# Counting the first pair of node tiles inside the preparation block of a graph network kernel

## The chip, the cores and the metric

The kernel runs on one NeuronCore of a Trainium2 chip. The time is device microseconds (us) of one launch, as the median of several runs. The five engines have their own instruction queues, each strictly in order: TensorE (PE in the profile; its weight loads are PEld), VectorE (DVE), ScalarE (ACT), GpSimd (POOL) and SyncE (SP, which here only starts DMAs). They meet at semaphores alone.

## The reference

6250 nodes with 256 features, 200000 edges sorted by destination, two graph-convolution layers and then a mixture of six experts (top 2). Cut to what the change touches:

```python
x = x + _L0_gnn_ref(_layernorm(x, axis=-1), edge_index, W, b, resW, resb)
...
deg = segment_sum(ones, dst); dis = rsqrt(deg); norm = dis[src] * dis[dst]   # self loops included
for l in range(2):
    h = x @ W[l]
    agg = segment_sum(norm[:, None] * h[src], dst) + b[l]
    x = relu(agg + x @ resW + resb)
```

## The kernel before, in words

The nodes are 49 tiles of 128 (`tiles`, padded to 50), taken two at a time as 25 `pairs`. The gather and the segment sum are done as a product of dense matrices: for each pair the kernel builds a matrix of edge counts (source node by destination node) and multiplies it with all messages, which stay in SBUF as two 16-bit parts (`parts`, a high part and the rest).

**The preparation block** (lines 755 to 1214, one `nc.Block`) does, for every tile `t` in two loops of 49, the work before the first layer's sums.

- The residual loop. VectorE gets the row statistics of a group of tiles (`stats`), ScalarE subtracts the mean in place (`centre`, L852), TensorE turns the tile (`turn`, L934), ScalarE copies it back (`turned_copy`, L862), TensorE multiplies with the residual weight (`residual`, L942) into one of four PSUM banks, and VectorE scales and stores it (`residual`, L1038). TensorE's tile `t` waits for VectorE's tile `t - 4`.
- The message loop. TensorE multiplies the turned tile with the layer's weight (`message`, L953, four PSUM banks), ScalarE writes the high part (`high`, L879), VectorE the rest (`rest_of`, L1045), ScalarE that rest as the second part (`middle`, L883). TensorE's message `t` waits for VectorE's `rest_of(t - 4)`.
- The keys. GpSimd fetches each tile's edge list by 49 indirect DMAs (L835). VectorE makes float keys in five batches of ten tiles, each in six steps (`key_step(n, step)`, L1058 to L1073; step 2 lets TensorE turn them, step 5 gives the node degrees). TensorE turns them pair by pair (`turn_keys`, L963), ScalarE copies them out as `keys_t` (`keys_copy`, L866) and takes the roots of the degrees (`roots`, L870, the first one in ScalarE's iteration 36).

All of this stands in a hand-written order: lists such as `STATS_AFTER`, `KEYS_AFTER_RES` (key batches 0 and 1 turned after residuals 34 to 38 and 44 to 48), `KEYS_AFTER_H` (batches 2 to 4 after messages 9, 17 and 27 on), `NORMS_BEFORE`, `FLAG_AFTER_H` say behind which tile a step is queued. `flag_and_bounds` is a chain of some 18 tiny VectorE instructions after `rest_of(37)`.

**The counting block** (`count_and_sum`, L1476 on) follows after a block boundary at which all engines meet. For each pair VectorE makes one-hot rows in 8 steps of 16 nodes (`rows_of_step`: a `rows_lo` and a `rows_hi` comparison, both at L623), TensorE counts them in 32 `quads` of four 128x98 matmuls (`build`, L1479), ScalarE copies each quad to `counts` (L1559). From the second pair on this runs beside the sums of the pair before (`sum_units`, L1404: 100 matmuls of 128x512 a pair). The first pair has nothing to run beside: its 32 quads stand ahead of the first sum.

The tile `counts` has two halves. In the preparation block the same memory holds the centred and turned features `feat`, so its first half comes free when message 24 is done.

Of the kernel before, what the change touches and what calls it, by code (L numbers as in the profile page):

```python
# [18 lines left out]
P = 128  # L19
# [460 lines left out]
def gnn_moe_kernel(nc, x, src, dst, gnn_w, gnn_b, res_w, res_b, router_w1, router_b1, router_w2, router_b2,  # L480
# [35 lines left out]
    with ctx:  # L516
# [92 lines left out]

        open_scope()  # L610
# [53 lines left out]
        assert 2 * pairs % BATCH == 0 and BATCH % 2 == 0  # L664

# [61 lines left out]
        middle_ready = sem("middle_ready")  # L727

# [4 lines left out]
        NORMS_BEFORE = 24  # L733
        STATS_AFTER = (16, 20, 26, 32)

        KEYS_AFTER_RES = (34, 44)
# [15 lines left out]
        def h_bank(t):  # L752
            return bank[(2, 3, 0, 1)[t % 4]]

# [3 lines left out]
        with nc.Block() as block:  # L758
# [39 lines left out]
            def _(pool):  # L798
# [14 lines left out]
                nc.gpsimd.iota(iota_hi[:, :, :], [[1, width], [0, 2]], 0, 0, allow_small_or_imprecise_dtypes=True)  # L813
# [35 lines left out]
            def _(act):  # L849
# [35 lines left out]

                act.wait_ge(cleared, 4)
# [4 lines left out]
                for t in range(tiles):  # L891
                    if t + 2 < tiles:
                        centre(t + 2)
                        if group_of(t + 2) != group_of(t + 1):
                            deviations(group_of(t + 2))
# [5 lines left out]
                    if t >= 4 and keys_after_res(t - 4) is not None:  # L901
                        keys_copy(keys_after_res(t - 4))
# [4 lines left out]
                for t in range(tiles - 4, tiles):  # L907
# [13 lines left out]
            def _(pe):  # L921
# [43 lines left out]

                count_heads(0)
# [23 lines left out]
                for t in range(tiles):  # L990
# [3 lines left out]
                    if t == FLAG_AFTER_H:  # L994
                        pe.wait_ge(disorder_ready, 1)
                        nc.tensor.matmul(bank[6][:, 0:3], ones[:, :], disorder[:, :], start=True, stop=True).then_inc(ones_summed, 1)

            @block.vector
            def _(dve):
# [135 lines left out]
                def flag_and_bounds():  # L1135
                    dve.wait_ge(ones_summed, 5)
                    link(nc.vector.tensor_reduce(over[:, 0:1], bank[6][:, 0:3], AX, ALU.add))
# [9 lines left out]
                    for l in range(layers):  # L1147
                        link(nc.vector.tensor_scalar(dis_back[:, l, :], dis[:, :], power[:, 1, l:l + 1].bitcast(F32), None, ALU.mult))

# [35 lines left out]
                for t in range(16, tiles):  # L1185
# [14 lines left out]
                for t in range(tiles):  # L1200
# [11 lines left out]
                    if t == 37:  # L1212
# [173 lines left out]
        QUAD = 4  # L1386
        quads = P // QUAD
        UNITS = 2 * (tiles + 1)
        LAST_UNITS = tiles + 1
        half_bank = 2  # L1390
# [1296 lines left out]
```

## Time and profile before

| | us |
|---|---|
| median of 3 runs (1899.73 to 1903.38) | 1903.04 |
| profiled execution | 1904.81 |
| its span in the trace | 1902.7 |
| residual loop starts, on TensorE | 18.79 |
| message loop starts, on TensorE | 120.49 |
| first counts matmul (pair 0) | 177.13 |
| first sum matmul of the first layer | 193.88 |

TensorE is busy for 1820.8 us, 96% of the span, VectorE for 1124.2 us, ScalarE for 853.7 us, GpSimd for 340.8 us. TensorE's granted clock, in tenths, over 40 slices of 47.6 us is 9988 and then 9 in all of the rest. A row of the view by stretch gives the busy time of each engine between two times, with the number of instructions in brackets, then the granted clock (1.00 is 2.4 GHz, 0.50 is 1.2 GHz), the busy share of the DMA engines and their GB/s. A row of the view in order of time gives start, length, engine, line, operation, tiles and shapes, how many instructions are merged in it, and in square brackets how long the engine sat idle before and what released it. A row of the groups by line gives the count, the busy time and the mean of one in ns.

### The profile page before, as it was taken

The numbers are of one execution on the slowest core, as the hardware profiler recorded it, in microseconds if no ns is written. First come the engines' busy times: TensorE is split into PE (matmuls) and PEld (weight loads), VectorE is DVE, ScalarE is ACT, GpSimd is POOL, SyncE is SP. The second block draws the span as 40 slices with busy tenths as digits, with TensorE's granted clock in tenths as the row PEclk, the third lists the DMA queues.
The fourth block names the chain that finished last, engine by engine and source line by source line (L and its number), as shares of the span: only waits on it lengthen the run. The fifth ranks groups of instructions, "written<-read, shape, count | busy, mean of one in ns | idle before, by whom it ended". The sixth has DMA issues, their size and how long they took to land. (4 is left out here: it accounts for less than half of the span.)

```text
span 1902.7 us, 35412 instructions
## 1 busy us (share of the span) xinstructions
PE 1820.8 (96%) x11170; PEld 1120.5 (59%) x11170; DVE 1124.2 (59%) x2789; ACT 853.7 (45%) x1822; POOL 340.8 (18%) x347
## 2 busy tenths in 40 slices
PE   4887999999999999999999999999999999999996
PEld 3666555555555555555544444444444478888885
DVE  7867666676666666766514444444444568555553
ACT  2567555555555555656512222222222232556562
POOL 1780000000000000000001111111111124333332
PEclk9988999999999999999999999999999999999998
DMA  7377999889999989898284555444445479324441
GB/s 216 99 129 133 327 300 318 288 289 284 292 286 288 257 305 347 328 323 306 104 338 179 190 179 188 179 179 179 179 179 182 180 232 335 111 77 122 141 135 55
DMA packets 135978, 416.70 MB, mean 219 GB/s; under 512 B 13685, under 2 KB 81611, under 8 KB 129640
## 3 DMA queue, kind: packets, MB, share of 16 engines
q1 hardware_dynamic: 90376, 255.13, 38.8%
q0 software_dynamic: 45392, 160.65, 28.8%
q8 instruction: 31, 0.51, 0.1%
q14 instruction: 35, 0.29, 0.1%
q10 hardware_dynamic: 144, 0.13, 0.0%
HBM read 162.27 MB, written 262.07 MB: 223 GB/s over the span
## 5 line engine op out<-in xcount | busy, mean ns | idle before, releaser
L1404 PE MATMUL bank<-parts,counts 128*128 128x512 f16 x4704 | 1158.4, 379 | 0.9 <-DVE sums L1425 0.9
L1404 PEld LDWEIGHTS bank<-parts,counts 128*128 128x128 f16 x4704 | 416.1, 97 | 358.0 <-issue 2.8
L1559 ACT ACTIVATE counts<-bank 128x392 f16<-128x392 f32 x800 | 394.7, 497 | 313.3 <-PE bank L1479 306.5
L623 DVE TENSOR_TENSOR rows<-rows,iota_lo 128x2048 bf16<-128x2048 bf16 x200 | 244.9, 1224 | 237.5 <-PE bank L1479 237.1
L1479 PEld LDWEIGHTS bank<-rows 128*128 128x128 bf16 x3200 | 229.7, 99 | 202.8 <-issue 27.6
L1479 PE MATMUL bank<-rows 128*128 128x98 bf16 x3200 | 280.5, 211 | 9.5 <-DVE rows L623 8.6
L623 DVE TENSOR_TENSOR rows<-rows,iota_hi 128x1568 bf16<-128x1568 bf16 x200 | 193.5, 968 | 0.0
L467 POOL DMA_INDIRECT first_rows<-route_rows,route_spot_i x49 | 47.8, 976 | 580.6 <-DVE tokens L458 405.0
L1419 ACT ACTIVATE middle<-bank 128x256 f32<-128x256 f32 x98 | 37.1, 380 | 187.0 <-PE bank L1404 172.2
L2187 PE MATMUL bank<-y_t,counts 128*128 128x256 f32 x480 | 114.4, 382 | 3.0 <-ACT y_t L2259 3.0
L2187 PE MATMUL bank<-h_t,counts 128*128 128x256 f32 x480 | 114.2, 381 | 0.0
L2216 PE MATMUL bank<-counts,h_t 128*128 128x256 f32 x480 | 113.5, 380 | 0.0
L2401 DVE TENSOR_SCALAR h_t<-bank,counts 128x256 f32<-128x256 f32 x120 | 57.8, 481 | 87.6 <-PE bank L2187 87.6
L2187 PEld LDWEIGHTS bank<-y_t,counts 128*128 128x128 f32 x480 | 91.3, 191 | 16.2 <-issue 3.7
L2263 ACT ACTIVATE h_t<-bank,counts 128x256 f32<-128x256 f32 x120 | 56.0, 467 | 98.5 <-PE bank L2187 89.0
L388 DVE TENSOR_TENSOR route_prob<-bank,router_b_sb 128x12 f32<-128x12 f32 (+1 forms) x25 | 4.2, 170 | 161.9 <-PE bank L378 161.9
L2216 PEld LDWEIGHTS bank<-counts,h_t 128*128 128x128 f32 x480 | 90.8, 190 | 12.2
L2288 ACT ACTIVATE counts<-parts 128x514 f32 x135 | 92.4, 700 | 9.0 <-issue 2.5
L2187 PEld LDWEIGHTS bank<-h_t,counts 128*128 128x128 f32 x480 | 87.2, 191 | 9.6
L183 PE MATMUL bank<-both_w,rows 128*128 128x512 f32 x196 | 92.2, 593 | 0.0
L2492 POOL DMA_INDIRECT first_out<-both_w,to_row x60 | 60.5, 1009 | 128.4 <-DVE both_w L2414 116.9
L2492 POOL DMA_INDIRECT out_dram<-both_w,to_row x60 | 58.3, 971 | 104.9 <-DVE both_w L2414 94.8
(268 smaller groups left out, 1761.1 us busy)
## 6 DMA issues: line engine op xcount, KB each, us to landing
counts_table<-counts SPq DMA_DIRECT2D x25, 3136.0 KB, 15.0
counts<-counts_table SPq DMA_DIRECT2D x24, 3136.0 KB, 11.7
first_rows<-zero_rows POOLq DMA_DIRECT2D x3, 10530.0 KB, 59.4
second_rows<-zero_rows POOLq DMA_DIRECT2D x3, 10449.0 KB, 69.6
first_out<-zero_rows POOLq DMA_DIRECT2D x3, 10368.0 KB, 50.5
res_tile<-res_table SPq DMA_DIRECT2D x98, 128.0 KB, 7.4
first_rows<-zero_rows POOLq DMA_DIRECT2D x1, 10270.0 KB, 60.4
second_rows<-zero_rows POOLq DMA_DIRECT2D x1, 10191.0 KB, 68.1
```

The costliest lines, as they stand in the source:

```text
L183: mm = nc.tensor.matmul(self.product_bank[:, :], self.x1_t[:, o, k * P:(k + 1) * P], self.both_w[:, self.l + 1, k, :], start=k == 0, stop= ...
L467: pool.indirect_dma_start(table, bass.IndirectOffsetOnAxis(ap=self.spot_i[:, b, c, o:o + 1], axis=0), rows[:, b, o, lo:hi], None, bounds_c ...
L623: return nc.vector.tensor_tensor(rows, k, v, ALU.is_equal)
L1404: mm = nc.tensor.matmul(acc[:, 0:2 * dim], lhs, rhs, start=s == 0, stop=s == tiles)
L1479: mm = nc.tensor.matmul(bank[4 + q % 4][:, u * width:(u + 1) * width], rows_lo[:, r % 2, at, :, u % 2], rows_hi[:, r % 2, at, :, u % 2], s ...
L1559: nc.scalar.activation(counts[:, b, :, :].rearrange("p s (o n) -> p o s n", o=2)[:, :, :, q * QUAD:(q + 1) * QUAD], bank[4 + q % 4][:, 0:Q ...
L2187: mm = nc.tensor.matmul(to[m][:, 0:ROWS], weights_of(k, n)[:, kf, m * P:(m + 1) * P], source[:, k % 2, kf, :], start=kf == 0, stop=kf == K ...
L2216: mm = nc.tensor.matmul(outs_bank[k % 2][:, cols_of], h2_t[:, k % 2, kf, h * P:(h + 1) * P], weights_of(k, 2)[:, kf, :], start=kf == 0, st ...
L2263: nc.scalar.activation(to[:, k % 2, 0, :], frm[0][:, 0:ROWS], ACT.Relu, bias=bias_of(k, n, 0)).then_inc(low_out, 1)
L2288: nc.scalar.activation(w[:, k % WB, part], held[:, bass.ds(e, 1), part].rearrange("p a n -> p (a n)"), ACT.Copy).then_inc(w_loaded[n][k % ...
L2401: nc.vector.tensor_scalar(to[:, k % 2, 1, :], frm[1][:, 0:ROWS], bias_of(k, n, 1), 0.0, ALU.add, ALU.max).then_inc(high_out, 1)
L2492: pool.indirect_dma_start(table, bass.IndirectOffsetOnAxis(ap=to_row[:, k % SB, h:h + 1], axis=0), result[:, k % 2, cols_of], None, bounds ...
```

## The change

The 32 quads of pair 0 move out of the counting block into the message loop of the preparation block: TensorE counts one or two of them behind each of the messages 25 to 45 into banks 6 and 7, ScalarE copies them between `high(t)` and `middle(t - 1)`, two messages later in TensorE's order than its own, and VectorE makes the eight one-hot steps behind `rest_of` of tiles 6, 14, 16, 24, 27, 30, 33, 36 (first comparison) and one tile later (second), in four buffers, two of them in the memory of edge lists that are no longer needed. In the counting block the copy loops begin with pair 1, and TensorE does 12 sum matmuls before the first quad of pair 1 (`SUMS_AHEAD`).

In the residual loop the key steps, the disorder check and the norms come three or four tiles earlier on VectorE, the turning of key batches 0 and 1 five tiles earlier on TensorE, and ScalarE's copy of turned keys, which stood behind `turned_copy(t)` four tiles later, stands two tiles later in front of `centre(t + 2)`. The flag's matmul goes to another bank and waits for the key copies; the flag's VectorE chain moves from behind tile 37 to behind tile 40. The amount of arithmetic is the same.

```diff
-        NORMS_BEFORE = 24
-        STATS_AFTER = (16, 20, 26, 32)
+        NORMS_BEFORE = 20
+        STATS_AFTER = (16, 20, 25, 31)
-        KEYS_AFTER_RES = (34, 44)
+        KEYS_AFTER_RES = (29, 39)
+        FREE_AFTER = -(-tiles // 2)
+        COUNT_FOR = tiles - FREE_AFTER - 3
+        AHEAD = 2
+        ROW_BUFS = 4
+        def quads_after(t):
+            return range(*(min(max(n, 0), COUNT_FOR) * quads // COUNT_FOR for n in (t - FREE_AFTER, t + 1 - FREE_AFTER)))
+        def quad_bank(q):
+            return bank[6 + q % 2]
+        ONEHOTS_AFTER_H = (6, 14, 16, 24, 27, 30, 33, 36)
...
# ScalarE
                 for t in range(tiles):
+                    if t >= 2 and keys_after_res(t - 2) is not None:
+                        keys_copy(keys_after_res(t - 2))
                     if t + 2 < tiles:
                         centre(t + 2)
...
-                    if t >= 4 and keys_after_res(t - 4) is not None:
-                        keys_copy(keys_after_res(t - 4))
...
                     high(t)
+                    if keys_after_h(t) is not None:
+                        keys_copy(keys_after_h(t))
+                    for q in quads_after(t + AHEAD):
+                        quad_copy(q)
                     if t >= 1:
                         middle(t - 1)
-                    if t >= 1 and keys_after_h(t - 1) is not None:
-                        keys_copy(keys_after_h(t - 1))
...
# TensorE
+                def count_quad(q):
+                    r, u0 = divmod(q * QUAD, STEP)
+                    if u0 == 0:
+                        pe.wait_ge(onehots_made, r + 1)
+                    if q >= 2:
+                        pe.wait_ge(quad_out, q - 1)
...
                     if t == FLAG_AFTER_H:
                         pe.wait_ge(disorder_ready, 1)
-                        nc.tensor.matmul(bank[6][:, 0:3], ones[:, :], disorder[:, :], start=True, stop=True).then_inc(ones_summed, 1)
+                        pe.wait_ge(keys_out, pairs - 1)
+                        nc.tensor.matmul(bank[5][:, 2 * P:2 * P + 3], ones[:, :], disorder[:, :], start=True, stop=True).then_inc(ones_summed, 1)
+                    for q in quads_after(t):
+                        count_quad(q)
...
# VectorE
+                def pair_heads(r):
...
+                    if r >= ROW_BUFS:
+                        dve.wait_ge(quad_ready, (r - ROW_BUFS + 1) * per_step)
+                    onehot_rows(lo_rows[r % ROW_BUFS], keys_t[:, 0, 1, r * STEP:(r + 1) * STEP], iota_lo, STEP, P)
+                def pair_tiles(r):
+                    onehot_rows(hi_rows[r % ROW_BUFS], keys_t[:, 0, 0, r * STEP:(r + 1) * STEP], iota_hi, STEP, width).then_inc(onehots_made, 1)
...
-                    if t == 22:
+                    if t == 18:
                         disorders()
-                    if t == 25:
+                    if t == 21:
                         norms()
-                    if 27 <= t < 33:
-                        key_step(0, t - 27)
-                    if 37 <= t < 43:
-                        key_step(1, t - 37)
+                    if 24 <= t < 30:
+                        key_step(0, t - 24)
+                    if 34 <= t < 40:
+                        key_step(1, t - 34)
...
+                    if t in ONEHOTS_AFTER_H:
+                        pair_heads(ONEHOTS_AFTER_H.index(t))
+                    if t - 1 in ONEHOTS_AFTER_H:
+                        pair_tiles(ONEHOTS_AFTER_H.index(t - 1))
-                    if t == 37:
+                    if t == 40:
                         flag_and_bounds()
...
# the counting block
+        SUMS_AHEAD = 12
...
                 def sum_pair(i, b, first, last=False):
                     pe.wait_ge(quad_out, i * quads + quads)
                     units = LAST_UNITS if last else UNITS
+                    ahead = SUMS_AHEAD if first else 0
+                    if first:
+                        sum_units(pe, b, i, i, 0, ahead, update.sums_out, update.sums_ready, first)
...
-                for q in range(quads):
-                    build(q, 0, True)
                 sum_pair(0, 0, True)
...
-                for i in range(4):
+                for i in range(1, 4):
                     pair(i, i % 2)
```

## Rows read from the trace of the kernel before

**Rows 1.** Busy time of each engine by stretch (us from the span's start)

```profile
64.60:97.00 32.40, 26.81 (x134) 20.76 (x132) 30.27 (x94) 16.50 (x44) 25.36 (x24) 1.00 0.36 104
92.00:120.50 28.50, 21.81 (x104) 17.43 (x102) 16.56 (x45) 11.90 (x35) 23.01 (x26) 0.82 0.35 96
121.00:150.00 29.00, 27.13 (x132) 22.01 (x131) 25.60 (x57) 22.61 (x65) 21.86 (x33) 1.00 1.06 140
177.00:193.50 16.50, 11.89 (x128) 10.20 (x128) 16.47 (x19) 13.33 (x32) 1.56 (x1) 0.50 0.90 253
193.50:198.00 4.50, 4.41 (x21) 2.20 (x22) 2.01 (x2) 1.49 (x3) 0.00 (x0) 0.50 1.01 259
193.00:1160.00 967.00, 964.02 (x6756) 523.42 (x6757) 587.08 (x1015) 489.87 (x1082) 65.17 (x39) 1.00 0.83 274
```

**Rows 2.** Order of time on PE: end of the residual loop, first messages

```profile
98.99 0.41 PE L963 MATMUL bank<-ident,node_keys 128*128 128x128 f32 x2 [4.17 <-ACT keys_t L866]
...
111.22 1.03 PE L942 MATMUL bank<-both_w,counts 128*128 128x256 f32 x4
112.08 0.38 PE L934 MATMUL bank<-ident,counts 128*128 128x128 f32 x2
112.30 1.03 PE L942 MATMUL bank<-both_w,counts 128*128 128x256 f32 x4
...
120.49 8.94 PE L953 MATMUL bank<-both_w,counts 128*128 128x256 f32 x40
```

**Rows 3.** Order of time on ACT: what it waits for at tile 36

```profile
97.03 0.21 ACT L870 ACTIVATE dis<-deg 128x10 f32<-128x10 f32 x1 [4.39 <-DVE deg L1073]
```

**Rows 4.** Order of time on DVE: rest of tile 24, the flag's chain

```profile
149.10 0.48 DVE L1045 SCALAR_TENSOR_TENSOR rest<-bank,message_scale,parts 128x256 f32<-128x256 f32 x1
...
161.83 0.15 DVE L1137 TENSOR_REDUCE over<-bank 128x1 f32<-128x3 f32 x1
...
165.39 0.88 DVE L1045 SCALAR_TENSOR_TENSOR rest<-bank,message_scale,parts 128x256 f32<-128x256 f32 x2
```

**Rows 5.** Order of time on ACT: one message, the last one, first quads

```profile
167.56 0.47 ACT L879 ACTIVATE parts<-bank,message_scale 128x256 f16<-128x256 f32 x1
167.91 0.41 ACT L883 ACTIVATE parts<-rest 128x256 f16<-128x256 f32 x1
168.23 0.46 ACT L879 ACTIVATE parts<-bank,message_scale 128x256 f16<-128x256 f32 x1
...
173.30 0.42 ACT L883 ACTIVATE parts<-rest 128x256 f16<-128x256 f32 x1 [0.25 <-DVE rest L1045]
177.67 1.67 ACT L1559 ACTIVATE counts<-bank 128x392 f16<-128x392 f32 x4 [3.95 <-PE bank L1479]
```

**Rows 6.** Groups by line, 0 to 320 us: copies of turned keys

```profile
L866 ACT ACTIVATE keys_t<-bank 128x256 bf16<-128x256 f32 x25 | 9.3, 376 | 1.7 <-PE bank L963 1.7
```

**Rows 7.** Order of time on DVE: start of the counting block

```profile
174.70 0.23 DVE L1523 COPY rows<-keys_t 128x256 bf16<-128x256 bf16 x1 [1.43 <-PEq L758]
174.96 1.23 DVE L623 TENSOR_TENSOR rows<-rows,iota_lo 128x2048 bf16<-128x2048 bf16 x1
...
176.99 1.22 DVE L623 TENSOR_TENSOR rows<-rows,iota_lo 128x2048 bf16<-128x2048 bf16 x1
```

**Rows 8.** Order of time on PE: last messages, first sums, a later quad

```profile
165.93 6.31 PE L953 MATMUL bank<-both_w,counts 128*128 128x256 f32 x28 [1.59 <-DVE rest L1045]
...
193.88 1.48 PE L1404 MATMUL bank<-parts,counts 128*128 128x512 f16 x3
...
210.54 0.35 PE L1479 MATMUL bank<-rows 128*128 128x98 bf16 x4
210.72 0.81 PE L1404 MATMUL bank<-parts,counts 128*128 128x512 f16 x3
```

**Rows 9.** One line's durations on DVE (min/median/max ns): two key steps

```profile
L1063 DVE TENSOR_TENSOR node_keys<-edge_hi,node_base x5: 815/815/817, 88.4 to 143.2; 128x640 f32<-128x640 int32 x5
L1058 DVE TENSOR_SCALAR key_i<-onehot_lo x5: 480/482/609, 87.1 to 141.7; 128x640 int32<-128x640 int32 x5
```

More of the change, by code:

```diff
@@ L608, in rows_of @@
             return table.rearrange("(t p) d -> p t d", p=P)
+        QUAD = 4
+        quads = P // QUAD
+        STEP = 16
+        steps = P // STEP
+        per_step = STEP // QUAD
         open_scope()
@@ L883, in middle, with quad_copy @@
                     nc.scalar.activation(parts[:, t, dim:2 * dim], rest[:, t % 2, :], ACT.Copy, scale=LOW).then_inc(middle_ready, 1)
+                def quad_copy(q):
+                    act.wait_ge(quad_ready, q + 1)
+                    nc.scalar.activation(
+                        counts[:, 0, :, :].rearrange("p s (o n) -> p o s n", o=2)[:, :, :, q * QUAD:(q + 1) * QUAD],
+                        quad_bank(q)[:, 0:QUAD * width].rearrange("p (n o s) -> p o s n", o=2, s=tiles), ACT.Copy).then_inc(quad_out, 1)
                 act.wait_ge(cleared, 4)
@@ L906, in _ @@
                         roots(1)
-                for t in range(tiles - 4, tiles):
+                for t in range(tiles - 2, tiles):
                     if keys_after_res(t) is not None:
@@ L964, in turn_keys @@
                     tr.then_inc(keys_turned, 1)
+                def count_quad(q):
[4 more added lines that the diff above has]
+                        pe.wait_ge(quad_out, q - 1)
+                    for u in range(QUAD):
+                        at = (u0 + u) // 2
+                        mm = nc.tensor.matmul(quad_bank(q)[:, u * width:(u + 1) * width], lo_rows[r % ROW_BUFS][:, at, :, u % 2],
+                                              hi_rows[r % ROW_BUFS][:, at, :, u % 2], start=True, stop=True)
+                    mm.then_inc(quad_ready, 1)
                 count_heads(0)
@@ L1136, in flag_and_bounds @@
                     dve.wait_ge(ones_summed, 5)
-                    link(nc.vector.tensor_reduce(over[:, 0:1], bank[6][:, 0:3], AX, ALU.add))
+                    link(nc.vector.tensor_reduce(over[:, 0:1], bank[5][:, 2 * P:2 * P + 3], AX, ALU.add))
                     link(nc.vector.tensor_scalar(over[:, 0:1], over[:, 0:1], 1.0, None, ALU.min))
@@ L1469, in tensor, with build @@
             def tensor(pe):
-                def build(q, i, first):
+                def build(q, i):
                     r, u0 = divmod(q * QUAD, STEP)
@@ L1474, in build @@
                         pe.wait_ge(onehots_made, i * steps + (r + 1))
-                    if not (first and q < 4):
-                        pe.wait_ge(quad_out, i * quads + (q - 3))
+                    pe.wait_ge(quad_out, i * quads + (q - 3))
                     for u in range(QUAD):
@@ L1509, in vector, with rows_of_step @@
             def vector(dve):
-                def rows_of_step(r, i, b, first):
-                    if not (first and r < 2):
-                        dve.wait_ge(quad_ready, i * quads + (r - 1) * per_step)
+                def rows_of_step(r, i, b):
+                    dve.wait_ge(quad_ready, i * quads + (r - 1) * per_step)
                     nodes_of = slice(r * STEP, (r + 1) * STEP)
@@ L1524, in pair @@
                                           keys_t[:, bass.ds(i, 1), :, :].rearrange("p a k n -> p (a k n)")).then_inc(keys_copied, 1)
-                    dve.wait_ge(keys_copied, i + 1)
+                    dve.wait_ge(keys_copied, i)
                     for r in range(steps):
-                        rows_of_step(r, i, b, isinstance(i, int) and i == 0)
+                        rows_of_step(r, i, b)
                         if there(i * 2 - 4):
@@ L1595, in pair @@
                                 update.high_part(act, i * 2 - 2, 0, i - 1)
-                for i in range(4):
+                for i in range(1, 4):
                     pair(i, i // 2, i % 2)
```

30 lines of the change are left out of this document (19 added, 11 removed).

## The prediction

> **What bounds the kernel now.** I read the stretches first [rows 1]. From 193 to 1160 us TensorE is busy for 964 of 967 us. Nothing in the change touches what stands there, so whatever the change gains or loses ahead of the first sum, which starts at 193.88 [rows 8], should appear unchanged at the end. The question is therefore only when the first sum can start. Ahead of it are three pieces with different limits.
>
> The residual loop ends at 120.49, where the first message starts [rows 2]. From 64.60 to 97.00 VectorE is busy for 30.27 of 32.40 us: it is the bound there, TensorE with 26.81 is not [rows 1]. Then comes a hold that belongs to nobody's work: TensorE sits idle 4.17 us for a copy of turned keys by ScalarE [rows 2], and ScalarE itself sat 4.39 us for the degrees of key batch 0, which VectorE makes behind tile 32 [rows 3]. After that hold the granted clock is low; over 92.0 to 120.5 it is 0.82 on average and TensorE is busy for only 21.81 of 28.50 us [rows 1].
>
> The message loop takes from 120.49 to 173.72, the end of ScalarE's last part (173.30 plus 0.42 [rows 5]). In its first half TensorE (27.13 of 29.0) and VectorE (25.60) are both nearly full [rows 1].
>
> The third piece is pair 0's counts. The counting block starts for VectorE at 174.70 [rows 7], 0.98 after ScalarE's end, and the first sum comes at 193.88. In it VectorE is busy for 16.47 of 16.50 us and TensorE runs at clock 0.50 [rows 1]. That is the piece that the change takes apart.
>
> **Residual loop: earlier by 8.1 us.** The same VectorE instructions stand ahead of tile 32 in both orders, so the full stretch of 30.27 us cannot shrink by more than its 2.1 us of idle time; I let VectorE finish tile 32 at 96 instead of 97. TensorE, which may lead by four tiles, is then at tile 36. The degrees of batch 0 are now made behind tile 29, seven tiles ahead of ScalarE's root at 36 and further back than TensorE's lead, so the 4.39 us hold goes; what is late next is VectorE, until 96. The key copy now stands two iterations behind its turning, ahead of `turned_copy`, so TensorE's next turning of keys no longer waits for a copy that itself waits for TensorE. Queued behind the copy on ScalarE are `centre` and `turned_copy`; their tiles are two ahead of the residual that wants them. From tile 36 on TensorE has 13 residuals with their turning, 1.08 us each (111.22 to 112.30 [rows 2]), 14.0 us, and five key turnings at 0.22 us (a turning, 112.08 to 112.30 [rows 2]), 1.1 us: 111.1 us. I add 1.3 us, because TensorE waits for batch 0's keys once behind tile 29 (an estimate of 2 to 3 us, since VectorE has disorders, norms and two groups of statistics close together there), and such a wait may lower its clock for a while. Messages start at 112.4 instead of 120.49: 8.1 us. Bounds: 10, if the clock never falls; 3, if the clock falls as it did behind the 4.17 us hold and all ten key tiles run slowly.
>
> **Message loop, first half: later by 4.4 us.** Until `rest_of(24)` three one-hot steps are added, 2.03 us each (174.96 to 176.99 [rows 7]), 6.1 us, on an engine that had 3.4 us idle in 29 [rows 1]. Half of that idle time I let them fill: 6.1 less 1.7 is 4.4. So `rest_of(24)`, which started 28.6 us behind the first message (149.10 [rows 4]), starts 33.0 us behind it. Bounds 2.7 (all idle time filled) and 6.1 (none). The fourth step's first half, 1.23 us, already lies beside the next piece.
>
> Here a rule speaks against the change. The rows: GpSimd issues DMAs for 21.86 us of 121 to 150 [rows 1], and the VectorE comparison with two SBUF inputs that is in the trace there, L1063, takes 815 to 817 ns in all five places, while the one-input L1058 goes from 480 to 609 [rows 9]. The Trainium skill ("SBUF — State Buffer", Who interferes with whom and SBUF: two separate sides) says that VectorE and GpSimd share a port pair that is locked for a whole instruction, and that a VectorE instruction with two SBUF inputs is blocked by a GpSimd one that reads SBUF. If each of the six one-hot instructions waited for one GpSimd instruction (21.86 / 33, 0.66 us), this half would be 4 us longer; by L1063 it is nothing, and I take nothing.
>
> **Message loop, second half: later by 7.9 us.** Here ScalarE becomes the bound. One message costs it 0.67 us (167.56 to 168.23 [rows 5]): 24 messages, 16.1 us. The 32 quad copies cost 1.67 / 4 = 0.42 us each [rows 5], 13.4 us. Five key copies of 0.376 us [rows 6] that overlap by a tenth make 1.4 us. The flag's chain holds VectorE for 3.56 us (161.83 to 165.39 [rows 4]) behind tile 40; ScalarE has two messages with three or four quads queued that do not need it, so I count 1.6 us of it. Sum 32.5 us from `rest_of(24)` to the last part, against 173.72 less 149.10, 24.6 us: 7.9 more. TensorE needs 0.89 us a message (8.94 us for ten [rows 2]) and about 1.5 quads of 0.18 us (210.54 to 210.72 [rows 8]), 1.17 us against ScalarE's 1.31, and it runs two messages ahead. VectorE needs 0.4 us plus a one-hot step every third tile, about 1.1 us. So both are cover, not bound; each quad waits for the copy two before it, which ScalarE made one message earlier. The steps for buffers 4 to 7 wait for quads counted at least one message before. Bounds: 5 (VectorE's flag hidden, TensorE's lead intact) and 12, below.
>
> **The block boundary and the first sum: earlier by 19.2 us.** ScalarE ends at 173.7 - 8.1 + 4.4 + 7.9 = 177.9; 0.98 us later, at 178.9, the counting block starts. TensorE now has 12 sums in front, which need no one-hot rows: at 1.48 / 3 or 0.81 / 3 us each [rows 8] 5.9 or 3.2 us, longer than the 0.26 + 2.03 = 2.3 us until pair 1's first rows [rows 7]. So the first sum starts at 178.9 instead of 193.88, and everything behind it is the same work. Its first 4.5 us ran at clock 0.50 [rows 1]; after an idle boundary of two to three us I expect the same again, worth at most 2.2 us if not.
>
> **The sum.** -8.1 + 4.4 + 7.9 - 19.2 = -15.0 us. The profiled execution took 1904.81 us, 1.77 above the median; 1904.8 - 15.0 = 1889.8, and against the median 1903.04 - 15.0 = 1888.0 us. I predict 1888.
>
> **Rivals.** (a) *The hold only moves.* The residual loop stays bound by waits on keys, gaining 3 of 8 us, or the one-hot steps fill no idle time and cost 6.1. For it: 30.27 of 32.40 us on VectorE [rows 1] leave little room. Time 1890 to 1896, about 1893.
> (b) *Quads and copies take turns.* If TensorE cannot get ahead of ScalarE, each quad and its copy stand in series: 32 x (0.18 + 0.50) + 21 x 0.89 = 40.5 us for messages 25 to 45 where the forecast has about 29; 11.5 more, 1899.5, no measurable change. Against it: two banks, and copies placed two messages behind.
> (c) *TensorE's clock stays low in the message loop* (slower than before). Behind the hold of 4.17 us [rows 2] the clock was low for so long that 92.0 to 120.5 averages 0.82 [rows 1], and messages with quads also leave it a little idle. At 1.2 GHz a message takes about 1.75 us and a quad 0.37 (11.89 / 32 [rows 1]); messages 25 to 48 take 24 x 1.75 + 32 x 0.37 = 54 us instead of 32.5, and 1888 + 21 = 1909. It decides from 15 such messages on: each costs 1.75 + 0.56 - 1.31 = 1.0 us, and 15 us is the gain. Against it: at 26.81 busy of 32.40 us the clock was still 1.00 [rows 1], and a slow TensorE would run without gaps.
> (d) *More than forecast:* all idle time filled, no low clock, the flag hidden: 1880 to 1884.
> (e) That the change doesn't do what it says, pair 0's quads still being counted behind the boundary, is excluded by the diff: the loop over them is gone.
>
> **Chances.** Forecast (1884 to 1892) 0.50; (a) 0.19; (d) 0.13; (b) 0.08, split between no change and its neighbours; (c) 0.10. A measurement can tell about 0.2%, 3.8 us. Faster 0.82, same 0.08, slower 0.10. Range: the forecast with (a) and (d) and the bounds above, 1880 to 1897, leaves (b), (c) and little else out.
>
> **What would show it.** In the profile after: no wait of TensorE on `keys_t` above 1 us and the first message at 110 to 115; ScalarE without idle time from message 25 on, with the quad copies between its two parts; the first sum at 176 to 183, at most 1.5 us behind VectorE's key copy; and from there to the end the same length as before, 1708.8 us. Wrong would be: TensorE waiting in every quad for a copy (b), a granted clock under 0.9 over the message loop (c), or a first sum that comes early while the sums of pair 0 wait for one-hot rows.

## The result and the profile after

The changed kernel takes 1891.09 us (median of 4 runs, 1889.59 to 1892.94), beside 1902.87 us for the kernel before on the same chip: a ratio of 0.9941, 95% interval 0.993 to 0.9953. It is 11.8 us faster, 3 us less than the 15 us of the sum. The time alone does not choose between the forecast (1884 to 1892) and rival (a) (1890 to 1896), since it lies in both; the marks below do. The profiled execution took 1892.94 us with a span of 1890.8 us, against 1904.81 and 1902.7 before.

The first reading is a list of marks on TensorE, in us from the start of each span. "First half" runs from the first message to VectorE's `rest_of(24)`, "second half" from there to the end of ScalarE's last part; the last column is the end of the last sum of both layers.

| | first message | first half | second half | first sum | last sum | span |
|---|---|---|---|---|---|---|
| before | 120.49 | 28.61 | 24.62 | 193.88 | 1539.94 | 1902.7 |
| forecast | 112.4 | 33.0 | 32.5 | 178.9 | | |
| after | 114.47 | 32.52 | 36.18 | 184.24 | 1528.32 | 1890.8 |

So the first sum comes 9.6 us earlier, and the sums themselves take 1344.1 us instead of 1346.1: 9.6 + 2.0 = 11.6 us at the last sum. The remaining 0.3 us lie behind it.

Busy time of each engine by stretch of after (columns: span of the stretch; busy us and instructions of PE, PEld, DVE, ACT, POOL; granted clock; DMA share; GB/s). The stretches are the residual loop up to tile 36, its end, the two halves of the message loop, and the boundary with the first sums; they answer to [rows 1].

```profile
64.98:98.90 33.92, 28.24 (x134) 21.71 (x132) 30.50 (x95) 18.29 (x52) 26.17 (x26) 0.95 0.34 102
99.00:114.50 15.50, 15.33 (x85) 13.09 (x86) 11.80 (x27) 9.62 (x28) 11.77 (x13) 1.00 0.47 145
114.50:147.00 32.50, 30.44 (x144) 22.40 (x143) 31.09 (x62) 22.68 (x63) 27.77 (x41) 1.00 0.96 151
147.00:183.20 36.20, 29.30 (x215) 23.45 (x213) 24.86 (x55) 30.51 (x86) 0.00 (x0) 0.95 0.33 50
183.20:188.70 5.50, 4.46 (x31) 2.34 (x32) 4.36 (x5) 1.02 (x3) 3.44 (x1) 1.00 0.70 293
```

Line 2 is the part that went best: TensorE busy for 15.33 of 15.50 us at full clock, where before the 28.5 us ahead of the first message had a clock of 0.82. In line 3 both TensorE and VectorE (31.09 of 32.50) are full. Line 4 is the surprise: no engine is full. ScalarE, which the sum took for the bound, is busy for 30.51 of 36.20 us.

TensorE in order of time, after (start, length, line, tiles; in brackets the idle time before and its releaser):

```profile
66.28 2.07 PE L983 MATMUL bank<-both_w,counts 128*128 128x256 f32 x4 [1.12 <-ACT counts L895]
...
83.91 1.10 PE L983 MATMUL bank<-both_w,counts 128*128 128x256 f32 x4 [2.50 <-DVE parts L1094]
...
90.50 0.44 PE L1004 MATMUL bank<-ident,node_keys 128*128 128x128 f32 x2 [2.02 <-DVE node_keys L1121]
...
99.12 1.10 PE L983 MATMUL bank<-both_w,counts 128*128 128x256 f32 x4 [0.26 <-DVE parts L1094]
...
114.47 9.04 PE L994 MATMUL bank<-both_w,counts 128*128 128x256 f32 x40
...
151.21 0.41 PE L1004 MATMUL bank<-ident,node_keys 128*128 128x128 f32 x2 [0.90 <-ACT keys_t L899]
...
153.52 0.41 PE L1004 MATMUL bank<-ident,node_keys 128*128 128x128 f32 x2 [0.79 <-ACT keys_t L899]
...
156.12 0.41 PE L1004 MATMUL bank<-ident,node_keys 128*128 128x128 f32 x2 [0.89 <-ACT keys_t L899]
...
175.53 2.08 PE L994 MATMUL bank<-both_w,counts 128*128 128x256 f32 x4 [2.25 <-DVE rest L1101]
...
184.24 2.76 PE L1475 MATMUL bank<-parts,counts 128*128 128x512 f16 x12 [2.93 <-PEq L791]
```

The 4.17 us hold on `keys_t` of [rows 2] is gone from the residual loop. A shorter wait on `keys_t` has appeared three times in the message loop. Message 45 waits 2.25 us for VectorE and then runs four matmuls in 2.08 us, twice the 1.09 that its neighbours take: half clock.

ScalarE in order of time, after, at the same places:

```profile
151.84 0.50 ACT L921 ACTIVATE counts<-bank 128x392 f16<-128x392 f32 x1 [0.77 <-PE bank L1015]
...
154.15 0.89 ACT L921 ACTIVATE counts<-bank 128x392 f16<-128x392 f32 x2 [0.77 <-PE bank L1015]
...
156.75 0.50 ACT L921 ACTIVATE counts<-bank 128x392 f16<-128x392 f32 x1 [0.77 <-PE bank L1015]
...
175.50 0.42 ACT L916 ACTIVATE parts<-rest 128x256 f16<-128x256 f32 x1 [1.24 <-DVE rest L1101]
...
177.97 0.89 ACT L921 ACTIVATE counts<-bank 128x392 f16<-128x392 f32 x2 [1.68 <-PE bank L1015]
...
182.75 0.42 ACT L916 ACTIVATE parts<-rest 128x256 f16<-128x256 f32 x1 [0.24 <-DVE rest L1101]
```

And VectorE, after: a one-hot step beside GpSimd's DMA issues, `rest_of(24)`, the flag's chain from its first instruction to the next rest, and the key copy that opens the counting block:

```profile
123.71 1.21 DVE L629 TENSOR_TENSOR pair_lo<-keys_t,iota_lo 128x2048 bf16<-128x2048 bf16 x1
...
146.99 0.48 DVE L1101 SCALAR_TENSOR_TENSOR rest<-bank,message_scale,parts 128x256 f32<-128x256 f32 x1
...
171.42 0.15 DVE L1193 TENSOR_REDUCE over<-bank 128x1 f32<-128x3 f32 x1
...
174.99 0.88 DVE L1101 SCALAR_TENSOR_TENSOR rest<-bank,message_scale,parts 128x256 f32<-128x256 f32 x2
...
184.14 0.23 DVE L1587 COPY rows<-keys_t 128x256 bf16<-128x256 bf16 x1 [1.43 <-PEq L791]
```

### The profile page after: what moved, and what is told of

Same layout as the page of the kernel before. It is cut to its first block and busy times, and to the rows that moved or that the text cites. A ratio compares the mean times of both kernels' runs of the same rounds, so it can differ in the third digit from the quotient of the medians.

```text
span 1890.8 us, 35393 instructions
## 1 busy us (share of the span) xinstructions
PE 1817.2 (96%) x11170; PEld 1115.8 (59%) x11170; DVE 1124.5 (59%) x2788; ACT 852.4 (45%) x1822; POOL 340.2 (18%) x347
## 5 line engine op out<-in xcount | busy, mean ns | idle before, releaser
L1623 ACT ACTIVATE counts<-bank 128x392 f16<-128x392 f32 x768 | 381.7, 497 | 305.4 <-PE bank L1543 298.0
L629 DVE TENSOR_TENSOR rows<-rows,iota_lo 128x2048 bf16<-128x2048 bf16 x192 | 235.3, 1225 | 232.1 <-PE bank L1543 231.6
L1543 PEld LDWEIGHTS bank<-rows 128*128 128x128 bf16 x3072 | 219.0, 98 | 190.7 <-issue 26.8
L1543 PE MATMUL bank<-rows 128*128 128x98 bf16 x3072 | 267.9, 208 | 0.1
L629 DVE TENSOR_TENSOR rows<-rows,iota_hi 128x1568 bf16<-128x1568 bf16 x192 | 186.0, 969 | 0.0
L2478 DVE SCALAR_TENSOR_TENSOR both_w<-bank,rows,both_w 128x256 f32<-128x256 f32 x120 | 52.5, 479 | 43.5 <-PE bank L2280 40.9
```

What stands on the lines that cost most here:

```text
L629: return nc.vector.tensor_tensor(rows, k, v, ALU.is_equal)
L1543: mm = nc.tensor.matmul(bank[4 + q % 4][:, u * width:(u + 1) * width], rows_lo[:, r % 2, at, :, u % 2], rows_hi[:, r % 2, at, :, u % 2], s ...
L1623: nc.scalar.activation(counts[:, b, :, :].rearrange("p s (o n) -> p o s n", o=2)[:, :, :, q * QUAD:(q + 1) * QUAD], bank[4 + q % 4][:, 0:Q ...
L2478: ins = nc.vector.scalar_tensor_tensor(result[:, k % 2, cols_of], outs_bank[k % 2][:, cols_of], rows[:, k % SB, h, gate_at[c]:gate_at[c] + ...
```

## What was still open

Three questions followed from these rows. First, what each half of the change earns alone. Second, why the second half took 36.18 us where 32.5 were forecast. My theory was two separate loops. One is a **key loop**: TensorE turns the keys behind message t + 2 only when the copy of the turning two messages back is out, that copy stands in ScalarE's iteration t, and behind it ScalarE waits for quads that TensorE counts behind that same turning. The other is the **flag's chain**: VectorE's 3.57 us from 171.42 to 174.99 is not covered, as ScalarE's 1.24 and 1.68 us of idle time show. The rival was one common cause, TensorE too slow or its lead too short for all quads (rival (b) of the prediction). Third, why the residual loop gained 6.0 us and not 8.1.

## Experiments on the two halves of the change

**Residual loop alone.** The kernel before, with only the new places of the residual loop: the lists, the key steps, the disorder check and the norms, and the key copy:

```diff
-        NORMS_BEFORE = 24
-        STATS_AFTER = (16, 20, 26, 32)
-        KEYS_AFTER_RES = (34, 44)
+        NORMS_BEFORE = 20
+        STATS_AFTER = (16, 20, 25, 31)
+        KEYS_AFTER_RES = (29, 39)
...
+                    if t >= 2 and keys_after_res(t - 2) is not None:
+                        keys_copy(keys_after_res(t - 2))
...
-                    if t >= 4 and keys_after_res(t - 4) is not None:
-                        keys_copy(keys_after_res(t - 4))
...
-                    if 27 <= t < 33:
-                        key_step(0, t - 27)
+                    if 24 <= t < 30:
+                        key_step(0, t - 24)
...
```

> The kernel before with only the new order of the residual loop (keys, norms, disorder check, key copies); pair 0 is still counted behind the block boundary. Theory: the parts add up; in the profile of the changed kernel the first message starts at 114.47 us instead of 120.49, so this kernel should start its messages at about 114.5 and be 6 us faster (4 to 8), about 1897. Rival: the 6 us only move, because the message loop then waits for key batches or for stores; then the messages start early but the first sum stays near 194 and the time near 1903.

Measured: 1896.69 us, ratio 0.9964 (0.9951 to 0.9977). The first message comes at 110.94, the first sum at 186.35.

**Counting alone.** The changed kernel with these places set back:

```diff
-        NORMS_BEFORE = 20
-        STATS_AFTER = (16, 20, 25, 31)
-        KEYS_AFTER_RES = (29, 39)
+        NORMS_BEFORE = 24
+        STATS_AFTER = (16, 20, 26, 32)
+        KEYS_AFTER_RES = (34, 44)
...
```

> The changed kernel with the residual loop in the order of before (keys turned after tiles 34 and 44, copied four tiles later). Theory: the parts add up; first message near 120.5, from there to the first sum 69.8 us as in the changed kernel, first sum near 190.3, time 1897, 6 us faster than before. Rival: the keys of batch 1, turned only at the end of the residual loop, delay the one-hot steps or the flag, and little of the gain is left, 1900 or more.

Measured: 1897.83 us, ratio 0.9967 (0.9954 to 0.998); first message 117.02, first sum 185.60.

On this chip the kernel before took 1903.93 us, so the halves earn 7.2 and 6.1 us, 13.3 together, where the whole change earned 11.8; the difference lies inside the intervals. Both are real and neither needs the other. The times came as expected, the marks did not: the first message was expected at 114.5 and 120.5, and came 3.6 and 3.5 us earlier. Two sizes in them are not what the order alone would give. In the residual-only kernel the first message gained 9.6 us, 1.5 of them ahead of tile 16 (61.89 instead of 63.43), where no order was changed. The boundary behind it grew: from the end of ScalarE's last part to VectorE's key copy it is 3.00 us (164.16 to 167.16) instead of 0.98. The idle time is put down to TensorE's sequencer, and its cause was not followed. In the count-only kernel, whose residual loop has the old order, the loop was still 2.7 us shorter than in before from tile 16 on, where the hold on `keys_t` was 2.60 us and the clock behind it fell less (0.93 over 92.0 to 117.0). So a comparison of single stages by one execution is uncertain by 2 to 3 us where the clock moves.

**The key copy's place.** The changed kernel with that copy back behind `turned_copy`, four tiles later:

```diff
-                    if t >= 2 and keys_after_res(t - 2) is not None:
-                        keys_copy(keys_after_res(t - 2))
...
+                    if t >= 4 and keys_after_res(t - 4) is not None:
+                        keys_copy(keys_after_res(t - 4))
```

> The changed kernel with ScalarE's copy of turned keys back at its old place, behind the copy of the turned tile four tiles later; all earlier placings stay. Theory: TensorE's next turning of keys again waits for a copy that itself waits for TensorE, about 0.8 us at six of the ten key tiles, and with gaps at each tile the clock may fall: the first message 3 to 6 us later than 114.5, the time 3 to 6 us above the changed kernel. Rival: the hold of before came from ScalarE's root of the degrees alone, which the earlier key steps already removed; then within 1.5 us of the changed kernel.

Measured: 1896.36 us, ratio 0.9961 (0.9947 to 0.9975); first message 118.80. TensorE in order of time in this kernel, three of the turnings of batch 1:

```profile
108.91 0.41 PE L1004 MATMUL bank<-ident,node_keys 128*128 128x128 f32 x2 [0.84 <-ACT keys_t L899]
...
111.24 0.41 PE L1004 MATMUL bank<-ident,node_keys 128*128 128x128 f32 x2 [0.84 <-ACT keys_t L899]
...
113.58 0.41 PE L1004 MATMUL bank<-ident,node_keys 128*128 128x128 f32 x2 [0.84 <-ACT keys_t L899]
```

There are six waits of 0.84 us, 5.0 us in all, and the first message is 4.3 us later than in after. The new place of the copy is therefore worth over half of what the residual loop gained; the hold of 4.17 us is gone here too, so that one fell to the earlier key steps. The wait of 0.84 is also in the kernel before, three times behind the long hold: it is what a copy costs that waits behind `turned_copy`, which itself waits for TensorE.

**No sums ahead of the first quad of pair 1.**

```diff
-        SUMS_AHEAD = 12
+        SUMS_AHEAD = 0
```

> The changed kernel without the 12 sums ahead of the first quad of pair 1. Theory: TensorE then waits 2.3 us more for pair 1's first one-hot rows, and the longer idle time also lowers its granted clock to 0.50 for some 4 us, as in the kernel before (which the changed kernel did not show): 2.3 plus about 2.2, 4.5 us slower than the changed kernel, near 1895.5. Rival: the clock stays at 1.00 either way; then 2.3 us, near 1893.4. Second rival: the rows were ready when TensorE was; then no difference.

Measured: 1894.37 us, ratio 0.995 (0.9935 to 0.9965), 3.3 us more than after. TensorE in order of time, this kernel:

```profile
186.33 0.49 PE L1543 MATMUL bank<-rows 128*128 128x98 bf16 x4 [5.22 <-DVE rows L629]
186.62 1.48 PE L1475 MATMUL bank<-parts,counts 128*128 128x512 f16 x3
...
188.23 1.23 PE L1475 MATMUL bank<-parts,counts 128*128 128x512 f16 x3
...
189.48 0.81 PE L1475 MATMUL bank<-parts,counts 128*128 128x512 f16 x3
```

TensorE waits for pair 1's first rows; the first sum is at 186.62 instead of 184.24, 2.4 us later (the prediction counted 2.3 for these rows), and six sums behind it take 2.71 instead of 1.62 us at half clock. Those 12 sums do what the sum of the prediction supposed. By the ratios the difference in time is 1.7 us, inside the intervals; the reading rests on the rows.

## Experiments on the second half of the message loop

All are the changed kernel with one to three edits. The marks are those of the first table, so each edit's place can be seen at once:

| | first message | first half | second half | first sum | last sum | median | ratio |
|---|---|---|---|---|---|---|---|
| after | 114.47 | 32.52 | 36.18 | 184.24 | 1528.32 | 1891.09 | 0.9941 |
| lag of one message | 111.07 | 32.13 | 32.00 | 176.24 | 1521.76 | 1888.25 | 0.9927 |
| keys earlier | 111.80 | 35.70 | 32.00 | 180.54 | 1526.32 | 1891.08 | 0.9942 |
| flag spread | 112.14 | 32.35 | 33.23 | 178.79 | 1525.32 | 1889.60 | 0.9932 |
| keys earlier, flag spread | 111.02 | 34.55 | 29.36 | 176.01 | 1521.55 | 1887.41 | 0.9926 |
| lag of one, flag spread | 112.63 | 32.35 | 30.38 | 176.40 | 1520.25 | 1885.33 | 0.9907 |
| after, again | 114.23 | 32.52 | 36.16 | 183.96 | 1528.04 | 1891.92 | 0.9936 |
| lag of one, flag spread, one-hots later | 112.88 | 31.86 | 30.19 | 176.00 | 1520.39 | 1886.17 | 0.9906 |

Two cautions for this table. The kernel before took 1902.87 us beside its first row, 1901.05 beside the next four and 1904.21 beside the last three, so the ratios compare and the medians do not. Their intervals are some 0.0013 to either side: by these intervals alone only the two kernels with a lag of one and the flag spread stand apart from after. And the marks are of one execution each: that of after took 1.9 us more than its median, that of the lag of one 1.8 us less than its own. The first message also moves with tile 16, which started at 61.8 to 63.8 us in kernels that are alike up to there. What an edit does is therefore read from the lengths of the two halves and from the waits in them.

**Lag of one message.** In its iteration t ScalarE copies the quads of message t + 1 instead of t + 2, so it asks for quads that stand in front of the turning behind message t + 2, not behind it. Its own parts then lag one message behind the quads instead of two:

```diff
-        AHEAD = 2
+        AHEAD = 1
```

> The changed kernel with ScalarE copying the quads of message t+1 instead of t+2 in its step t. Theory: the waits of 0.8 to 0.9 us behind messages 28 to 31 (TensorE's key turning waits for the key copy of two messages before, which stands in the same ScalarE step that then waits for quads behind that turning) are a loop of order, not of work; with one message less of lag they vanish, 2.5 to 3 us off the 36.2 us between the rest of tile 24 and the last part. Rival: with less lead each quad then waits for the copy two before it, TensorE idles through messages 25 to 45, and the stage gets no shorter or some us longer.

Measured: 1888.25 us, ratio 0.9927 (0.9913 to 0.994). ScalarE in order of time over the iterations with key copies, this kernel:

```profile
147.81 0.41 ACT L899 ACTIVATE keys_t<-bank 128x256 bf16<-128x256 f32 x1
148.08 0.53 ACT L921 ACTIVATE counts<-bank 128x392 f16<-128x392 f32 x1
...
149.12 0.43 ACT L899 ACTIVATE keys_t<-bank 128x256 bf16<-128x256 f32 x1
149.38 0.94 ACT L921 ACTIVATE counts<-bank 128x392 f16<-128x392 f32 x2
...
150.79 0.47 ACT L899 ACTIVATE keys_t<-bank 128x256 bf16<-128x256 f32 x1
151.06 0.59 ACT L921 ACTIVATE counts<-bank 128x392 f16<-128x392 f32 x1
```

No quad copy here has a wait any more, and the second half is 4.2 us shorter. No wait of ScalarE from 140 us to its last part is above 0.5 us but one, 1.64 us at the flag (168.56), where after had 1.24 and 1.68. The expected gain was 2.5 to 3 us. The three waits at key copies in after add up to 2.3 us; of the other 1.9 us, 1.3 are saved at the flag (1.24 + 1.68 - 1.64), and 0.6 were not followed. The key loop is confirmed: the lag, not a lack of speed, was the cause, since no engine has less to do here.

**Keys earlier.** The same loop avoided in another way: batches 3 and 4 are turned before quads begin:

```diff
-        KEYS_AFTER_H = (9, 17, 27)
+        KEYS_AFTER_H = (9, 14, 19)
...
-                    if 18 <= t < 24:
-                        key_step(4, t - 18)
+                    if 14 <= t < 20:
+                        key_step(4, t - 14)
```

> The changed kernel with key batches 3 and 4 turned behind messages 14 and 19 instead of 17 and 27 and batch 4 made by VectorE behind tiles 14 to 19 instead of 18 to 23, so that no key turning lies between quads. Theory (the same loop, taken away from its other side): ScalarE's four waits of 0.77 us vanish, 2.5 to 3 us less than the changed kernel, if VectorE's first half gets no longer. Rival: VectorE's steps for tiles 14 to 19 and the one-hot steps there pile up and delay the first half by as much.

Measured: 1891.08 us, ratio 0.9942 (0.9928 to 0.9956): no gain in the time. The second half is 32.00, again 4.2 us shorter, but the first half is 3.2 us longer. Busy time and TensorE in order of time where that went, this kernel:

```profile
131.00:143.00 12.00, 9.61 (x34) 6.85 (x33) 11.72 (x21) 6.61 (x20) 11.05 (x17) 0.72 1.09 120
```

```profile
134.22 1.13 PE L994 MATMUL bank<-both_w,counts 128*128 128x256 f32 x4 [1.02 <-DVE rest L1101]
136.64 0.69 PE L1004 MATMUL bank<-ident,node_keys 128*128 128x128 f32 x2 [1.28 <-DVE node_keys L1121]
137.12 1.91 PE L994 MATMUL bank<-both_w,counts 128*128 128x256 f32 x4
```

VectorE is busy for 11.72 of 12.00 us: the key steps of two batches and the one-hot steps now stand close together. TensorE waits for them twice, and behind the waits its clock falls (four matmuls in 1.91 us). What stood in one half has moved to the other, as the rival in the expectation had it.

**Flag spread.** The same VectorE instructions of the flag, in nine pieces of one or two behind tiles 38 to 46:

```diff
...
-                    if t == 40:
-                        flag_and_bounds()
+                    if 38 <= t < 47:
+                        flag_step(t - 38)
```

> The changed kernel with the flag's chain of 17 VectorE instructions spread in nine pieces behind tiles 38 to 46 instead of in one piece behind tile 40. Theory: the hold of 3.56 us stops everybody for longer than the 1.6 us of the prediction (TensorE 2.25 us, ScalarE 1.24 and 1.68 us, and a lowered clock behind it); spread, it hides in VectorE's gaps, 2.5 to 4 us less than the changed kernel, no wait above 0.5 us on the rest of tiles 41 to 44. Rival: the chain's length counts wherever it lies, 1 us or less.

Measured: 1889.60 us, ratio 0.9932 (0.9918 to 0.9946). The second half is 33.23, 2.95 us shorter. TensorE at message 45 (first row) and the last three messages behind it, this kernel:

```profile
170.63 1.09 PE L994 MATMUL bank<-both_w,counts 128*128 128x256 f32 x4
...
172.04 2.17 PE L994 MATMUL bank<-both_w,counts 128*128 128x256 f32 x8
174.52 1.13 PE L994 MATMUL bank<-both_w,counts 128*128 128x256 f32 x4 [0.31 <-DVE rest L1101]
```

The wait of 2.25 us and the message at half clock are gone; ScalarE's three waits behind key copies (0.77, 0.78, 0.78 us) are still there. The two causes are separate. In time the gain is some 1.5 us where 2.5 to 4 were expected, too little to tell from none.

**Keys earlier and flag spread together.**

> Keys earlier and flag spread together. Theory: both holds are separate, so 5 to 7 us less than the changed kernel, about 1885; from message 25 on ScalarE has no wait above 0.5 us until its last parts. Rival: what one removes the other already covers (TensorE's lead), then no more than the better of the two.

Measured: 1887.41 us, ratio 0.9926 (0.9912 to 0.994). Both effects are in the table: second half 29.36, first half 34.55. The 5 to 7 us expected did not come in the time, since the longer first half takes 2 us of it.

**Lag of one and flag spread together.**

> The changed kernel with ScalarE's quad copies one message behind instead of two and the flag's chain spread. Theory: the loop through the key turning and the flag's hold are separate; 62.5 to 64.5 us from the first message to the first sum where the changed kernel had 69.8 and lag 1 alone 65.2; 1885 to 1887. Rival: with lag 1 the flag's hold was already mostly covered (TensorE's wait there 1.24 us), no better than lag 1 alone, 1888.

Measured: 1885.33 us, ratio 0.9907 (0.9893 to 0.9921), the best of all. On the same chip the changed kernel, unaltered, took 1891.92 us (ratio 0.9936, 0.9922 to 0.9949), so the two edits are worth 6.6 us more. The second half took 30.38 us; with the lag of one alone it took 32.00, so at this lag the flag costs 1.6 us. With the flag spread in both, the lag alone is worth 2.85 us (33.23 to 30.38), near the 2.3 us of the three waits. Busy time over this second half, columns as above:

```profile
144.98:175.36 30.38, 27.88 (x215) 22.29 (x213) 23.80 (x55) 29.72 (x85) 0.00 (x0) 1.00 0.43 73
```

ScalarE is busy for 29.72 of 30.38 us: without the two loops it is the bound that the prediction took it for.

**The changed kernel again.**

> The changed kernel once more, unaltered, beside the next two, so that differences of 2 to 5 us are read against it. Theory: the granted clock in the stretch ahead of the sums differs from one execution to the next (tile 16 of the residual loop started at 61.8 to 63.8 us in kernels that are the same up to there, and at tile 17 the clock was low in some and full in others); so this profile's residual loop should differ from the first one's by up to 2 us with the same program, the median 1889 to 1893.

Measured: every mark within 0.3 us of after, the fall of the clock at residual tile 17 included. The expectation that two executions of this program would differ by up to 2 us in the residual loop missed. But both profiled executions lie above the medians (1892.94 over 1891.09, 1892.57 over 1891.92), so it is not shown that the clock falls at tile 17 in every run.

**One-hot steps later.** The kernel with both edits, with the steps of VectorE's full first half moved back:

```diff
-        ONEHOTS_AFTER_H = (6, 14, 16, 24, 27, 30, 33, 36)
+        ONEHOTS_AFTER_H = (6, 20, 25, 28, 31, 34, 37, 40)
```

> The same as lag 1 with the flag spread, and VectorE's one-hot steps placed behind tiles 6, 20, 25, 28, 31, 34, 37, 40 instead of 6, 14, 16, 24, 27, 30, 33, 36, so that one step and a half less lies in the first half of the message loop. Theory: the first half is paid for on VectorE instruction by instruction, so it is 2 to 3 us shorter up to the rest of tile 24, and VectorE's gaps behind ScalarE hide the moved steps; 2 to 3 us less than the kernel with lag 1 and the flag spread. Rival: the rows then come late for the quads and TensorE waits for them behind messages 28 to 44; no gain or a loss.

Measured: 1886.17 us, ratio 0.9906 (0.9892 to 0.992): no different from the kernel without this edit, where 2 to 3 us less were expected. The first half lost only 0.5 us. VectorE is still crowded in one place: the one-hot step behind tile 20 falls among the key steps of batch 4, which stand behind tiles 18 to 23. ScalarE in order of time, this kernel, waiting for VectorE there:

```profile
140.75 0.42 ACT L916 ACTIVATE parts<-rest 128x256 f16<-128x256 f32 x1 [1.34 <-DVE rest L1101]
...
142.55 0.42 ACT L916 ACTIVATE parts<-rest 128x256 f16<-128x256 f32 x1 [1.03 <-DVE rest L1101]
```

## Why the prediction was right, and where its sum was wrong

**The bound** was read rightly. From the first sum to the last of both layers it is the same work: 1346.06 us before, 1344.08 after, and in all thirteen profiled executions (before, after, eleven experiments) between 1343.85 and 1346.53. What is won ahead of the first sum does reach the end.

**Residual loop, -8.1 forecast, -6.0 measured.** The hold went. The one wait of 2 to 3 us for batch 0's keys came (2.02), and ahead of it one of 2.50 us that was not counted, for a residual tile that VectorE stored only behind its norms. From tile 36 to the first message it took 15.35 us, where 15.1 were counted and 1.3 allowed on top. The term that was wrong is VectorE's end of tile 32: 96 was assumed and 98.9 came (the first of three in the last row below). VectorE's work was 30.50 us beside 30.27 before, but it waited twice for TensorE. VectorE in order of time, after:

```profile
70.27 0.48 DVE L1094 SCALAR_TENSOR_TENSOR parts<-bank,rstd,bias_sum 128x256 f32<-128x256 f32 x1 [1.30 <-PE bank L983]
...
75.81 0.48 DVE L1094 SCALAR_TENSOR_TENSOR parts<-bank,rstd,bias_sum 128x256 f32<-128x256 f32 x1 [0.82 <-PE bank L983]
...
98.50 1.26 DVE L1094 SCALAR_TENSOR_TENSOR parts<-bank,rstd,bias_sum 128x256 f32<-128x256 f32 x3
```

TensorE was late because its clock had fallen to half at tile 17 (66.28: four matmuls in 2.07 us, behind 1.12 us of idle time). In the kernels with the same residual order in which it did not fall there, tile 16 to first message takes 49.05 to 49.33 us instead of 50.66: with before's 57.06 that is 7.7 to 8.0 us, the forecast. So the order is worth what was predicted and the clock took 1.6 us of it; another 0.4 lie ahead of tile 16 (63.81 instead of 63.43). The match of the order with the forecast is in part luck. VectorE in order of time in the kernel with both edits, where the clock did not fall:

```profile
96.64 1.26 DVE L1094 SCALAR_TENSOR_TENSOR parts<-bank,rstd,bias_sum 128x256 f32<-128x256 f32 x3
```

There too VectorE ends tile 32 at about 97, as before the change, and not at 96: it filled next to none of its idle time. Of the 1.3 us allowed on top 1.0 was not used, and that made up for it. Rival (a), that the hold only moves, did not hold: the loop gained 6.0 us and not 3, and no wait on `keys_t` is left in it.

**First half, +4.4 forecast, +3.9 measured.** VectorE filled idle time as assumed. The six one-hot instructions took 1.21 to 1.22 and 0.96 to 0.97 us beside GpSimd's DMA issues (27.77 us of them in this stretch), and 1.22 and 0.96 in the second half, where GpSimd does nothing (0.00). The rule that the prediction quoted from the Trainium skill ("SBUF — State Buffer", Who interferes with whom) asks for a GpSimd instruction that reads SBUF, and does not say that a DMA issue is one. In this trace the comparisons, with two SBUF inputs, were not held up, and taking nothing for it was right.

**Second half, +7.9 forecast, +11.6 measured.** This is the term that was mis-sized. The count of ScalarE's work was good: 32.5 less the 1.6 for the flag is 30.9, and the kernel without either loop took 30.38. What the sum left out is the order of the key turning, its copy and the quads, checked only for the banks and not for the wait on `keys_t`; so that loop stood at nothing. And the flag was counted at 1.6 us, because ScalarE had quads queued; but with a lag of two it soon asks for the quads behind message 45, which TensorE reaches only behind the flag (the 1.68 us wait, beside the 1.24 on the rest itself). With a lag of two the key loop cost 4.2 us with what hangs on it, the flag 2.95 by itself (the two overlap: together 5.8). That the flag costs 1.6 us at a lag of one is luck: the prediction counted it for a lag of two. Rival (b), a series of quads and copies throughout, would have made 11.5 more of this; the series existed, but only at the messages with a turning. Rival (c) did not come: the clock was 1.00 and 0.95 over the two halves.

**The boundary, -19.2 forecast.** From the end of ScalarE (183.17) to the key copy (184.14) it is again 0.97 us, the first sum follows 0.10 us later, and it no longer waits for rows. The step held; the first sum came late only by what stood ahead of it (114.47 - 112.4 = 2.1, then -0.5 and +3.7).

**The clock at the first sums** was taken as low, worth at most 2.2 us if not. It was full: 12 sums in 2.76 us, and the sums took 2.0 us less in all. So -6.0 + 3.9 + 11.6 - 19.1 - 2.0 = -11.6 us at the last sum. The forecast of 1888 was 3 us low, mainly by the second half. The first sum was 5.3 us later than forecast; the 2.0 us given back here were allowed for and not counted, and without them the time would have been nearer to 1893. Of the marks that the prediction set, the first message (110 to 115) and the absence of long waits on `keys_t` held; ScalarE without idle time did not, and so the first sum missed 176 to 183 by 1.2 us.

## What to carry to other kernels

When work is moved into a loop of several in-order engines, follow each new wait round the loop: an engine that copies result t + 2 and releases step t + 2 in the same iteration waits for itself, however idle all engines are, and a lag smaller by one can be faster. A chain of tiny instructions is best spread over iterations before one counts on a lead to cover it. And a stage that ends earlier earns its gain only if the copies and releases behind it stand ahead of what waits for the engine that was released.

## What the runs showed of the hardware

TensorE's clock came out differently at places that look alike. At residual tile 17 TensorE idles 1.11 to 1.12 us in all of these kernels, before included, behind 0.70 to 0.76 us at tile 16. The four matmuls then took 2.07 us (half clock) in after, in its repetition, without sums ahead and with the copy behind, and 1.13 us (full clock) in the others, as in the one with both edits, in order of time on TensorE:

```profile
63.57 1.13 PE L983 MATMUL bank<-both_w,counts 128*128 128x256 f32 x4 [0.76 <-ACT counts L895]
...
66.03 1.13 PE L983 MATMUL bank<-both_w,counts 128*128 128x256 f32 x4 [1.12 <-ACT counts L895]
```

The same holds for the first 12 sums. Behind an idle boundary of 2.93 us they took 2.76 us in after (full clock); behind one of 3.14 us they took 2.76 us with both edits but 5.29 us with the flag spread alone:

```profile
178.79 5.29 PE L1489 MATMUL bank<-parts,counts 128*128 128x512 f16 x12 [3.14 <-PEq L791]
```

All five executions with full clock there (after and its repetition, the copy behind, both edits, one-hots later) needed 1343.9 to 1344.4 us from first to last sum, the eight others 1344.7 to 1346.5. What decides between the two was not found. Behind the last sum, the rest of the program took 362.5 to 363.2 us in ten profiled executions, but 360.6, 364.7 and 365.0 in three, in code that no edit touched. Differences under 2 us between two of these kernels are therefore not explained here; the 6.6 us between the changed kernel and the one with both edits stands in the medians of five runs each.
